# Where V's product and the gate's product of a span stand in TensorE's order, in a delta-rule layer on one core

## The chip, the cores and the metric

The kernel runs on one core of a Trainium2 chip. The metric is the device time of one execution in microseconds, as the median of several runs. A core has five engines with instruction streams of their own: TensorE (PE; its weight loads are PEld), VectorE (DVE), ScalarE (ACT), GpSimd (POOL) and SyncE (SP), which here only issues DMAs. They meet through semaphores alone.

## The reference, cut to what matters

The input is 16 sequences of 512 tokens with 512 features. Four layers follow each other: a delta-rule attention layer, a feed-forward layer with routed adapters, a softmax attention layer, and the feed-forward layer again. The change touches the first only:

```python
q = silu(x @ Wq.T).reshape(b, n, h, hd)          # 16 heads of 32
k = silu(x @ Wk.T).reshape(b, n, h, hd)
v = (x @ Wv.T).reshape(b, n, h, hd)
beta = 2.0 * jax.nn.sigmoid(x @ Wbeta.T)
k = k * jax.lax.rsqrt(jnp.sum(k * k, axis=-1, keepdims=True) + EPS)
# for every token:  pred = kt S;  delta = bt (vt - pred);  S = S + kt delta;  o = qt S
o = _delta_rule(q, k, v, beta).reshape(b, n, d)
gate = jax.nn.sigmoid(x @ Wg1.T @ Wg2.T)
og = (o * gate).reshape(b, n, h, hd)
rms = jax.lax.rsqrt(jnp.mean(og * og, axis=-1, keepdims=True) + EPS)
og = (og * rms).reshape(b, n, d) * g_norm
return og @ Wo.T
```

## The kernel before, in words

**Tiling.** A sequence is cut into two spans of 256 tokens, so there are 32 spans. A span has four chunks of 64 tokens. The recurrence over tokens is rewritten: within a chunk, the dependence of later tokens on earlier ones is a triangular matrix per head (`triangles`, stored in `tri`), whose inverse is computed on VectorE in 32x32 blocks (`invert`). Between chunks only the state S is carried, in four steps per span (`chain(c)` on TensorE, `advance(c)` on VectorE).

**Software pipeline.** `over_spans` calls `begin` for the first two spans and then one `step` per span on every engine. In one step each engine works on several spans at once: `now` is solved and chained; `ahead`, the next, is inverted on VectorE; `further`, two spans on, is projected on TensorE; `beyond` is loaded and normalised; `behind` gets its output product. 28 of the steps are alike in that all of these exist and the pipeline is full. The order within a step is written out by hand for each engine, in the functions `step` of the kernel text. The products of 128x128 weights (k, q, V, output) are split into three products of reduced-precision parts (`split3`, lines 38 to 42), so that their instructions carry the lines L40 to L42 in the profile.

**TensorE's order before**, in one step: transposes of the normalised x (`turned`), `solve_first`, k's first half, `solve_second`, k's second half, `solve_third`, q's first half, `solve_fourth`, g and beta, `query_corrections`, output's first half, `transitions`, q's second half, `without_state`, output's second half, `state_inputs`, and then chain(0), key_sums(0), chain(1), gate(0), chain(2), gate(1), chain(3), key_sums(1), output_sums, V(0), key_rows, triangles, V(1). `key_sums` sums the squares of k by a product with ones, `output_sums` those of the gated output, and `key_rows` transposes the normalised k.

**What passes between the engines at the end of a step.** VectorE multiplies the output of each chain step by the gate (L918). ScalarE squares it (L366). TensorE sums (L701). ScalarE takes Ln (L371) and Exp (L376), and VectorE applies the result (L925, `output`). Then VectorE masks the triangles, eight of them (L883), and normalises x of `beyond` (L835), for which `turned` waits. TensorE's second set of four triangle products waits for VectorE, because it uses the same four banks. k's norm goes the same way: `key_sums`, Ln and Exp on ScalarE (`k_inverse_norms`, L329 and L333), the product on VectorE (`normalise_k`, L848), `key_rows` on TensorE.

**PSUM banks.** Eight banks of 512 columns. BA, BB, BC and BD (0 to 3) are shared by the transposes, the projections, the gate, V, key_sums, key_rows and the output product, banks 4 to 7 by the solve, the chain, output_sums and the triangles. A projection waits until the last user of its bank has been copied out.

**ScalarE's function tables.** Silu and Tanh are in one table set, Ln and Exp in another. The kernel loads each ahead of its first use (L433, L443), so that there are two loads a step. ScalarE's other work is copying and splitting: `x_hi` (L299) from the transposes, V and k rows into `rhs`, the solve's results into `uw`. VectorE takes `x_lo` (L841) from `x_hi`, and k's projection needs both.

**SyncE's order.** `store` and `load_residual`, then `from_lanes` (the inverted blocks go to DRAM, L207, and return in eight loads as `inv_b`, L211), then `to_lanes` (beta out, L190; eight stores of `tri`, L196; beta and blocks back into lanes, L200 and L202). The queue issues them in this order, and each waits for its own semaphore.

Of the kernel before, what the change touches and what calls it, by code (L numbers as in the profile page):

```python
# [44 lines left out]
def delta_rule_layer(nc, dims, x_in, w_main, w_gb, w_g2, g_norm, ident_in, masks_in, ones_in, out):  # L45
# [9 lines left out]
    with ExitStack() as ctx:  # L55
# [227 lines left out]
        def _(act):  # L283
# [99 lines left out]
            def begin(first, second, third):  # L383
                load_x(*first)
                act.wait_ge(xn_ready, TS)
                load_x(*second)
                for span, following in ((first, None), (second, third)):
                    if following:
                        act.wait_ge(xn_ready, 2 * TS)
                        load_x(*following)  # L390
                    act.preload_act_table_set(SILU_SET)
                    turned(*span)
                    take_k(*span, 0)
                    take_k(*span, 1)
# [3 lines left out]
                    take_gate(*span)  # L398
                    act.preload_act_table_set(LN_EXP_SET)
                    k_inverse_norms(*span)  # L400
                    take_v(*span, 0)
                    take_v(*span, 1)
                    take_k_rows(*span)
                act.preload_act_table_set(SILU_SET)

            def step(behind, now, ahead, further, beyond):
# [19 lines left out]
                if further:  # L426
                    take_q(*further, 1)
                output_squares(*now, 0)
                output_squares(*now, 1)
                if further:  # L430
                    act.wait_ge(og_ready, at(*now, 4, 4))
                    take_gate(*further)
                act.preload_act_table_set(LN_EXP_SET)  # L433
                if further:
                    k_inverse_norms(*further)
                output_inverse_rms(*now)
                if further:
                    take_v(*further, 0)
                output_hi(*now)
                if further:  # L440
                    take_k_rows(*further)
                    take_v(*further, 1)
                    act.preload_act_table_set(SILU_SET)  # L443

# [7 lines left out]
        def _(pe):  # L452
# [11 lines left out]
            def turned(b, s, first=False):  # L464

                pe.wait_ge(xn_ready, at(b, s, TS, TS))
                if not first:
                    pe.wait_ge(v_ready, at(b, s, TS, -1))
# [18 lines left out]
            def project_gb(b, s, first=False):  # L487
                if not first:
                    pe.wait_ge(v_ready, at(b, s, TS, 0))
                for k in range(KT):  # L490
# [232 lines left out]
            def begin(first, second, third):  # L723
                for span in (first, second):
# [5 lines left out]
                    project_q(*span, 1)  # L730
                    key_sums(*span, 0)
                    project_gate(*span, 0)
                    project_gate(*span, 1)
                    key_sums(*span, 1)
                    project_v(*span, 0)
                    project_v(*span, 1)
                    key_rows(*span)
# [5 lines left out]
            def step(behind, now, ahead, further, beyond):  # L743
# [28 lines left out]
                if further:  # L772
                    project_gate(*further, 0)
                chain(*now, 2)
                if further:
                    project_gate(*further, 1, behind)
                chain(*now, 3)
                if further:
                    key_sums(*further, 1)
                output_sums(*now)  # L780
                if further:
                    project_v(*further, 0)
                    key_rows(*further)
                    pe.wait_ge(ln2_ready, at(*now, 2, 2))
                    triangles(*further, 0)
                    triangles(*further, 1)
                    project_v(*further, 1)

# [8 lines left out]
        def _(dve):  # L797
# [156 lines left out]
            def step(behind, now, ahead, further, beyond):  # L954
# [30 lines left out]
                advance(*now, 3)  # L985
                invert_ahead("values")
                if further:
                    normalise_k(*further)
                output(*now)
                if further:  # L990
# [874 lines left out]
```

## Time and profile before

| | |
|---|---|
| median of 3 runs | 5666.98 us (5666.64 to 5681.62) |
| profiled execution | 5643.14 us, span 5641.2 us |
| mean granted TensorE clock | 0.936 |
| PE busy | 4965.0 us, 88% |
| DVE busy | 3602.9 us, 64% |
| ACT busy | 2445.5 us, 43% |
| POOL busy | 706.2 us, 13% |

Times are in microseconds from the start of the span. A granted clock of 1.00 is 2.4 GHz and 0.50 is 1.2 GHz. The shares are averages over the whole program. The layer in question ends at about 2,100 us.

### The profile page before, as it was taken

The numbers are of one execution on the slowest core, as the hardware profiler recorded it, in microseconds if no ns is written. First come the engines' busy times: TensorE is split into PE (matmuls) and PEld (weight loads), VectorE is DVE, ScalarE is ACT, GpSimd is POOL, SyncE is SP. The second block draws the span as 40 slices with busy tenths as digits, with TensorE's granted clock in tenths as the row PEclk, the third lists the DMA queues.
The fourth block names the chain that finished last, engine by engine and source line by source line (L and its number), as shares of the span: only waits on it lengthen the run. The fifth ranks groups of instructions, "written<-read, shape, count | busy, mean of one in ns | idle before, by whom it ended". The sixth has DMA issues, their size and how long they took to land.

```text
span 5641.2 us, 152483 instructions
## 1 busy us (share of the span) xinstructions
PE 4965.0 (88%) x62928; PEld 3566.3 (63%) x62928; DVE 3602.9 (64%) x7842; ACT 2445.5 (43%) x4660; POOL 706.2 (13%) x917
## 2 busy tenths in 40 slices
PE   4899999999999949898898898998988988988988
PEld 4787777777787736556556556555565565565565
DVE  3676676676676637566566565675675665665756
ACT  2333433333433324354363453553543644634535
POOL 0000000000000001111112112111111111121121
PEclk8899999999999969999999999998999999999999
DMA  1222222222322220000000000000000000000000
GB/s 55 67 56 68 70 56 67 71 56 63 74 56 68 66 73 1 16 2 16 16 1 16 16 1 16 16 1 16 1 16 16 2 16 16 1 16 17 1 16 9
DMA packets 352741, 173.61 MB, mean 31 GB/s; under 512 B 300033, under 2 KB 300801, under 8 KB 351265
## 3 DMA queue, kind: packets, MB, share of 16 engines
q1 hardware_dynamic: 343056, 146.25, 9.7%
q10 hardware_dynamic: 8976, 17.30, 1.0%
q8 instruction: 519, 8.50, 0.6%
q14 instruction: 190, 1.55, 0.1%
HBM read 94.79 MB, written 67.63 MB: 29 GB/s over the span
## 4 chain that ended last, share of the span: by engine, by line
issue 30%; PE 21%; DVE 7%; POOL 3%; ACT 1%; DMA 0%; DVEq 0%; POOLq 0%; SPq 0%; ACTq 0%
PE row_psum L40 5%; PE row_psum L42 5%; PE row_psum L41 5%; DVE smax L1772 3%; POOL xs L1227 2%; PE row_psum L1356 1%; PE row_psum L1493 1%; DVE stats L1598 1%; PE row_psum L1460 1%; POOL rstd L1199 1%; PE row_psum L1461 1%; PE row_psum L1475 1%; DVE xr_lo L1627 1%; DVE xs L1701 1%; DVE probs L1609 0%
## 5 line engine op out<-in xcount | busy, mean ns | idle before, releaser
L1772 DVE TENSOR_REDUCE smax<-row_psum 128x1 f32<-128x512 f32 x2048 | 1263.7, 683 | 294.7 <-PE row_psum L1493 293.4
L1325 ACT ACTIVATE probs<-row_psum 128x512 f32<-128x512 f32 x2048 | 1078.3, 610 | 528.5 <-PE row_psum L1506 350.0
L1493 PE MATMUL row_psum<-k_stack,q_stack 128*128 128x512 f32 x2048 | 866.6, 434 | 28.3 <-DVE smax L1772 24.5
L1506 PE MATMUL row_psum<-q_stack,k_stack 128*128 128x512 f32 x2048 | 855.2, 428 | 29.2 <-ACT probs L1325 20.9
L1493 PEld LDWEIGHTS row_psum<-k_stack,q_stack 128*128 128x128 f32 x2048 | 395.0, 194 | 346.3 <-DVE smax L1772 251.4
L1506 PEld LDWEIGHTS row_psum<-q_stack,k_stack 128*128 128x128 f32 x2048 | 385.9, 191 | 292.8 <-ACT probs L1325 188.6
L1519 PE MATMUL row_psum<-probs,v_aug 128*32 128x512 f32 x4096 | 489.1, 598 | 0.0
L40 PE MATMUL row_psum<-wf_hi,xr_hi 128*128 128x320 f32 (+1 forms) x1024 | 328.2, 321 | 13.1 <-DVE xr_lo L1627 12.5
L868 DVE TENSOR_TENSOR lane_t<-lane_t,lane_p 128x30 f32<-128x30 f32 (+14 forms) x960 | 318.5, 332 | 32.9
L865 DVE TENSOR_TENSOR lane_p<-lane_t 128x30 f32<-128x30 f32 (+14 forms) x960 | 316.2, 329 | 23.5
L40 PE MATMUL span_bank<-x_hi,w_hi 128*128 128x256 f32 x1024 | 301.0, 294 | 29.7 <-DVE x_lo L841 29.2
L42 PE MATMUL row_psum<-wf_hi,xr_lo 128*128 128x320 f32 (+1 forms) x1024 | 325.1, 317 | 0.0
L41 PE MATMUL row_psum<-wf_lo,xr_hi 128*128 128x320 f32 (+1 forms) x1024 | 324.3, 317 | 0.0
L1356 PE MATMUL row_psum<-ident,probs 128*128 128x128 f32 x784 | 169.5, 371 | 172.9 <-DVE probs L1609 172.8
L41 PE MATMUL span_bank<-x_lo,w_hi 128*128 128x256 f32 x1024 | 288.6, 282 | 0.0
L42 PE MATMUL span_bank<-x_hi,w_lo 128*128 128x256 f32 x1024 | 288.1, 281 | 0.0
L1762 DVE RECIPROCAL av_rc<-row_psum 128x16 f32<-128x16 f32 x128 | 32.2, 252 | 397.8 <-PE row_psum L1566 397.8
L1227 POOL TENSOR_TENSOR xs<-xs,av_n 128x256 f32<-128x256 f32 x128 | 92.9, 726 | 1538.5 <-DVE av_n L1766 1538.5
L1245 ACT ACTIVATE xr_hi<-row_psum 128x512 fp32r<-128x512 f32 x196 | 112.0, 600 | 398.6 <-PE row_psum L1356 398.6
L1356 PEld LDWEIGHTS row_psum<-ident,probs 128*128 128x128 f32 x784 | 119.8, 187 | 223.8 <-DVE probs L1609 173.0
L263 POOL TENSOR_TENSOR o_lo<-og_both,o_hi 128x512 fp32r<-128x512 f32 x64 | 93.2, 1475 | 1323.1 <-DVE tri L883 1233.5
L1519 PEld LDWEIGHTS row_psum<-probs,v_aug 128*32 128x32 f32 x4096 | 108.5, 109 | 218.0 <-issue 173.8
(207 smaller groups left out, 9955.2 us busy)
## 6 DMA issues: line engine op xcount, KB each, us to landing
xs<-x SPq DMA_DIRECT2D x17, 1024.0 KB, 5.6
x_sp<-in_x ACTq DMA_DIRECT2D x33, 512.0 KB, 3.9
tri_dram<-tri SPq DMA_DIRECT2D x256, 64.0 KB, 2.1
lane_t<-tri_dram SPq DMA_DIRECT2D x32, 512.0 KB, 4.7
inv_dram<-lane_t SPq DMA_DIRECT2D x32, 512.0 KB, 2.6
inv_b<-inv_dram SPq DMA_DIRECT2D x256, 64.0 KB, 2.3
x_res<-in_x SPq DMA_DIRECT2D x32, 512.0 KB, 3.8
x<-x_res SPq DMA_DIRECT2D x32, 512.0 KB, 3.7
```

Of the source, the lines that this page charges most:

```text
L40: pe.matmul(out, a_hi, b_hi, start=first, stop=False)
L41: pe.matmul(out, a_hi, b_lo, start=False, stop=False)
L42: return pe.matmul(out, a_lo, b_hi, start=False, stop=last)
L865: mark(dve.tensor_tensor(prod, lane_t[:, 0:m, m:m + 1].to_broadcast([P, m, n]), lane_t[:, m:m + 1, m + 1:NB].to_broadcast([P, m, n]), ALU. ...
L868: mark(dve.tensor_tensor(lane_t[:, 0:m, m + 1:NB], lane_t[:, 0:m, m + 1:NB], prod, ALU.add))
L1227: pool.tensor_tensor(xq, xq, av_n[:, :, :, :].rearrange("p t h e -> p t (h e)"), ALU.add).then_inc(adot_added, 1)
L1325: act.activation(probs[:, h % PROBS, tt, :], ps[:, m % STACK_BANKS, :], ACT.Exp, scale=float(DH) ** -0.5).then_inc(exp_ready, 1)
L1356: last = pe.transpose(ps[:, t, P * k:P * k + P], xn[:, t, P * k:P * k + P], ident2[:, :])
L1493: pe.matmul(ps[:, STACK_BANKS + m % MAX_BANKS, :], q_stack[:, qt, P * st:P * st + P], k_stack[:, kv, :], start=True, stop=True).then_inc(m ...
L1506: pe.matmul(ps[:, m % STACK_BANKS, :], k_stack[:, kv, P * tt:P * tt + P], q_stack[:, qt, :], start=True, stop=True).then_inc(score_mm, 1)
L1519: last = pe.matmul(ps[32 * e:32 * e + 32, 6, :], v_aug[:, tt, h % NKV, :], probs[:, h % PROBS, tt, :], start=tt == 0, stop=tt == NT - 1)
L1772: dve.tensor_reduce(smax[:, g, st:st + 1], ps[:, STACK_BANKS + (NT * g + st) % MAX_BANKS, :], AX.X, ALU.max).then_inc(max_ready, 1)
```

## The change

On TensorE, V(0) moves to the place between chain(1) and chain(2), and V(1) to the place between chain(2) and chain(3), with key_sums(1) ahead of it. gate(0) moves behind output_sums, ahead of key_rows, and gate(1) behind the triangles, to the end of the step. The waits that protect banks BA and BB go along: V now waits for q and beta, the gate for V's copies, and the next span's transposes and g product for the gate's. On ScalarE, the load of the Ln and Exp table, V's copies and k's norms stand between the squares of the output; the load of the Silu and Tanh table, the copies of the key rows and the gate's Tanh stand at the end. On VectorE, `normalise_k` stands ahead of the inversion's last columns (`values`, two columns and the scaling) and no longer behind them. In `begin` the order of V and gate changes likewise, on TensorE and ScalarE. No instruction is added or removed.

```diff
 # ScalarE, step
                 take_transition(*now)
                 if further:
                     take_q(*further, 1)
+                act.preload_act_table_set(LN_EXP_SET)
+                if further:
+                    take_v(*further, 0)
                 output_squares(*now, 0)
+                if further:
+                    k_inverse_norms(*further)
+                    take_v(*further, 1)
                 output_squares(*now, 1)
-                if further:
+                output_inverse_rms(*now)
+                output_hi(*now)
+                if further:
+                    act.preload_act_table_set(SILU_SET)
                     act.wait_ge(og_ready, at(*now, 4, 4))
+                    take_k_rows(*further)
                     take_gate(*further)
-                act.preload_act_table_set(LN_EXP_SET)
-                if further:
-                    k_inverse_norms(*further)
-                output_inverse_rms(*now)
-                if further:
-                    take_v(*further, 0)
-                output_hi(*now)
-                if further:
-                    take_k_rows(*further)
-                    take_v(*further, 1)
-                    act.preload_act_table_set(SILU_SET)
 # TensorE, waits
-            def project_gate(b, s, n, behind=None):
+            def project_gate(b, s, n):
+                pe.wait_ge(v_ready, at(b, s, TS, n + 1))
                 if n == 0:
-                    pe.wait_ge(q_ready, at(b, s, 2, 1))
                     pe.wait_ge(g1_ready, at(b, s, 1, 1))
-                else:
-                    pe.wait_ge(beta_ready, at(b, s, 1, 1))
-                    if behind:
-                        pe.wait_ge(x2_ready, at(*behind, TS, CREDIT + TS))
...
-            def project_v(b, s, t):
-                pe.wait_ge(gate_ready, at(b, s, 2, t + 1))
+            def project_v(b, s, t, behind=None):
+                if t == 0:
+                    pe.wait_ge(q_ready, at(b, s, 2, 1))
+                else:
+                    pe.wait_ge(beta_ready, at(b, s, 1, 1))
+                    if behind:
+                        pe.wait_ge(x2_ready, at(*behind, TS, CREDIT + TS))
 # TensorE, step
                 chain(*now, 1)
                 if further:
+                    project_v(*further, 0)
+                chain(*now, 2)
+                if further:
+                    key_sums(*further, 1)
+                    project_v(*further, 1, behind)
+                chain(*now, 3)
+                output_sums(*now)
+                if further:
                     project_gate(*further, 0)
-                chain(*now, 2)
-                if further:
-                    project_gate(*further, 1, behind)
-                chain(*now, 3)
-                if further:
-                    key_sums(*further, 1)
-                output_sums(*now)
-                if further:
-                    project_v(*further, 0)
                     key_rows(*further)
                     pe.wait_ge(ln2_ready, at(*now, 2, 2))
                     triangles(*further, 0)
                     triangles(*further, 1)
-                    project_v(*further, 1)
+                    project_gate(*further, 1)
 # VectorE, step
                 advance(*now, 3)
+                if further:
+                    normalise_k(*further)
                 invert_ahead("values")
-                if further:
-                    normalise_k(*further)
                 output(*now)
```

## Rows read from the trace of the kernel before

**Rows 1.** Windows of core 0: stretch and its length, then busy us of each engine.
```profile
core 0: us, PE busy (x) PEld busy (x) DVE busy (x) ACT busy (x) POOL busy (x), PEclk, DMA share, GB/s
213.23:1902.70 1689.47, 1594.74 (x41105) 1320.38 (x41105) 1184.77 (x2912) 643.57 (x1121) 107.46 (x113) 0.97 0.26 65
970.70:981.00 10.30, 10.30 (x214) 7.13 (x215) 3.98 (x14) 0.67 (x2) 0.00 (x0) 0.57 0.18 55
```
**Rows 2.** Waits from 400 to 1950 us: who waited for whom, total, times, longest.
```profile
PE span_bank L40 <- DVE x_lo L841: 22.0, 25, 1.2
...
PE span_bank L691 <- issue: 18.0, 14, 2.4
```
**Rows 3.** Timeline of TensorE from 1036.9: start, us, line, idle before and releaser.
```profile
1037.00 1.13 PE L524 MATMUL span_bank<-g_beta,g 32*128 32x256 f32 x4
...
1039.98 0.45 PE L685 MATMUL span_bank<-state,gt 32*32 32x32 f32 x32
1040.85 1.12 PE L511 MATMUL span_bank<-sq,head_ones 128*128 128x512 f32 x2
1042.10 1.12 PE L701 MATMUL span_bank<-og_both,head_ones 128*128 128x512 f32 x2
...
1047.49 1.09 PE L539 MATMUL span_bank<-ident,kq 128*128 128x128 f32 x8 [0.62 <-DVE kq L848]
1048.52 5.03 PE L551 MATMUL span_bank<-kq 32*64 32x128 f32 x128
1053.48 0.50 PE L40 MATMUL span_bank<-w_hi,x_hi 128*128 128x512 f32 x1
...
1056.75 1.09 PE L474 MATMUL span_bank<-ident,r_norm 128*128 128x128 f32 x8 [0.20 <-DVE r_norm L835]
...
1060.55 0.36 PE L40 MATMUL span_bank<-x_hi,w_hi 128*128 128x256 f32 x1 [0.81 <-DVE x_lo L841]
...
1068.44 0.24 PE L577 MATMUL span_bank<-og_both,inv_b 32*32 32x64 f32 x1
```
**Rows 4.** Timeline of VectorE from 1040.9 to 1064.2, same columns.
```profile
1040.96 0.42 DVE L918 SCALAR_TENSOR_TENSOR og_both<-gate,span_bank 128x256 f32<-128x256 f32 x1
...
1043.55 0.20 DVE L874 COPY lane_t<-lane_b 128x32 f32<-128x32 f32 x1
1046.14 1.29 DVE L848 TENSOR_TENSOR kq<-kq,r_norm 128x512 f32<-128x512 f32 x2 [2.40 <-ACT r_norm L333]
1048.34 1.67 DVE L925 SCALAR_TENSOR_TENSOR og_both<-og_both,gnorm_half 128x256 f32<-128x256 f32 x4 [0.90 <-ACT og_both L376]
1049.93 4.87 DVE L883 TENSOR_TENSOR tri<-span_bank,masks 128x512 f32<-128x512 f32 x8
1054.71 1.98 DVE L835 TENSOR_SCALAR r_norm<-x_sp,mv,rstd 128x512 f32<-128x512 f32 x2
...
1063.96 0.18 DVE L856 TENSOR_SCALAR lane_b<-lane_b 128x32 f32<-128x32 f32 x1 [3.55 <-DMA lane_t<-tri_dram]
```
**Rows 5.** Timeline of ScalarE from 1046.5 to 1059.6, same columns.
```profile
1046.52 1.26 ACT L371 ACTIVATE og_both<-span_bank,eps_t 128x512 f32<-128x512 f32 x2
1047.66 1.16 ACT L376 ACTIVATE og_both<-og_both 128x512 f32<-128x512 f32 x2
...
1057.19 1.28 ACT L443 ACT_TABLE_LOAD   x1
1058.49 1.09 ACT L299 ACTIVATE x_hi<-span_bank 128x512 fp32r<-128x512 f32 x2
```
**Rows 6.** Timeline of SyncE's DMA issues from 1043 to 1064.2, same columns.
```profile
1046.40 4.05 SPq L211 DMA_DIRECT2D inv_b<-inv_dram  x8
...
1052.43 4.39 SPq L196 DMA_DIRECT2D tri_dram<-tri  x8
...
1058.34 0.34 SPq L202 DMA_DIRECT2D lane_t<-tri_dram  x1
```
**Rows 7.** The tile lane_t from 400 to 1900 us: time from issue to landing.
```profile
DMA to landing us min/median/max: 2.6/3.1/5.8
```
**Rows 8.** Page, DMA queues: packets, MB, share of 16 engines' span.
```profile
q8 instruction: 519, 8.50, 0.6%
```

More of the change, by code:

```diff
@@ L397, in begin @@
                     take_q(*span, 1)
-                    take_gate(*span)
+                    take_v(*span, 0)
+                    take_v(*span, 1)
                     act.preload_act_table_set(LN_EXP_SET)
                     k_inverse_norms(*span)
-                    take_v(*span, 0)
-                    take_v(*span, 1)
                     take_k_rows(*span)
-                act.preload_act_table_set(SILU_SET)
+                    act.preload_act_table_set(SILU_SET)
+                    take_gate(*span)
             def step(behind, now, ahead, further, beyond):
@@ L427, in step @@
                     take_q(*further, 1)
-                output_squares(*now, 0)
-                output_squares(*now, 1)
-                if further:
-                    act.wait_ge(og_ready, at(*now, 4, 4))
-                    take_gate(*further)
                 act.preload_act_table_set(LN_EXP_SET)
                 if further:
+                    take_v(*further, 0)
+                output_squares(*now, 0)
+                if further:
                     k_inverse_norms(*further)
+                    take_v(*further, 1)
+                output_squares(*now, 1)
                 output_inverse_rms(*now)
-                if further:
-                    take_v(*further, 0)
                 output_hi(*now)
                 if further:
+                    act.preload_act_table_set(SILU_SET)
+                    act.wait_ge(og_ready, at(*now, 4, 4))
                     take_k_rows(*further)
-                    take_v(*further, 1)
-                    act.preload_act_table_set(SILU_SET)
+                    take_gate(*further)
             def end(now):
@@ L467, in turned @@
                 if not first:
-                    pe.wait_ge(v_ready, at(b, s, TS, -1))
+                    pe.wait_ge(gate_ready, at(b, s, 2, -1))
                     pe.wait_ge(rhs_k_ready, at(b, s, TS, 0))
@@ L488, in project_gb @@
                 if not first:
-                    pe.wait_ge(v_ready, at(b, s, TS, 0))
+                    pe.wait_ge(gate_ready, at(b, s, 2, 0))
                 for k in range(KT):
@@ L526, in project_gate @@
                 last.then_inc(gate_proj, 1)
-            def project_v(b, s, t):
-                pe.wait_ge(gate_ready, at(b, s, 2, t + 1))
+            def project_v(b, s, t, behind=None):
+                if t == 0:
+                    pe.wait_ge(q_ready, at(b, s, 2, 1))
+                else:
+                    pe.wait_ge(beta_ready, at(b, s, 1, 1))
+                    if behind:
+                        pe.wait_ge(x2_ready, at(*behind, TS, CREDIT + TS))
                 for k in range(KT):
@@ L731, in begin @@
                     key_sums(*span, 0)
+                    project_v(*span, 0)
+                    project_v(*span, 1)
+                    key_sums(*span, 1)
                     project_gate(*span, 0)
                     project_gate(*span, 1)
-                    key_sums(*span, 1)
-                    project_v(*span, 0)
-                    project_v(*span, 1)
                     key_rows(*span)
@@ L985, in step @@
                 advance(*now, 3)
-                invert_ahead("values")
                 if further:
                     normalise_k(*further)
+                invert_ahead("values")
                 output(*now)
```

2 lines of the change are left out of this document (1 added, 1 removed).

## The prediction

> **What bounds the kernel now.** I read the waits of the stretch in which the layer runs evenly, then one period of it engine by engine, then the granted clock. The slices of the page put the change's layer into the first 2,100 us; the token layers behind it are untouched. Its steady part is 28 periods, 1689.47 us, so 60.3 us each, with TensorE busy for 94% of it [rows 1]. TensorE sets the period: what the change can win or lose is TensorE idle time and its clock. The waits show two kinds of idle time that matter [rows 2]: x_lo ends late (22.0 us over 25 periods, about 0.8 each), and "issue" at the chain (18.0 us in 14). The rows of one period, counted from the start of chain(3) at 1039.98 (t = 0), show the rest [rows 3]: output_sums at 2.12, a wait of 0.62 for kq ahead of key_rows, triangles from 8.54 to 13.50, V1 behind them to 16.57, a wait of 0.20 for xn, and turned at 16.77. That last wait is small, but it says that VectorE reaches this point together with TensorE. VectorE's rows [rows 4] give its own course: last gated output ready at 1.40, inversion done at 3.77, a hole until ScalarE has k's norms, normalise_k, another hole until ScalarE has the output's norms, output at 8.36, tri from 9.95 to 14.8, xn until 16.71. So the stretch from chain(3) to turned is already a chain through VectorE with V0 and V1 lying beside it as cover.
>
> **TensorE, chain(3) to turned.** Each V takes 3.07 us (1053.48 to the wait before 1056.75), 3.0 from start to start; a gate product 1.1, key_sums 1.1 [rows 3]. V0, V1 and key_sums(1) leave this stretch (7.1 us), both gates enter it (2.2): 4.9 to 5.0 us less work. The same work goes between the chain's steps, where TensorE is busy anyway; it costs there what it costs here. So the sum is about idle time alone.
>
> **The course through VectorE.** New order: og(3) at 1.40, Square, output_sums at 2.12 as before (the 0.72 between them is the Square); its first sum is there at 3.24, its second at about 4.1. ScalarE is free now: the table load and k's norms ran before. Ln of half a tile is 1.26/2, Exp 1.16/2 [rows 5]: Ln to 3.9, Ln to 4.8, the first Exp to 5.4. VectorE meanwhile: normalise_k 1.29 (its norms are ready, because key_sums(1) stands before V1), inversion 2.4, done at 5.1. Output starts at 5.5 instead of 8.36, 2.9 earlier, and tri, xn and turned follow at the same distances: tri 1.59 later, its eight products 4.8, xn 2.0. Turned starts at 13.9 instead of 16.77. TensorE would be through with its part at 0.87 + 1.75 + 1.1 + 1.03 + 4.96 + 1.1, about 10.8. So it stands idle for 3.1 us here (1.25 right behind chain(3), which key_sums(1) covered, and 1.8 before turned, which V1 covered) where it stood for about 1.1. **Price: +2.0 us a period.** Bounds: 1.5 if the output's norms come 0.5 earlier than I have them (the inversion ends at 5.1, so not more), 2.5 if the extra wait between engines comes in twice.
>
> **x_lo.** The table load at 1057.19 goes ahead of x_hi because V1's copy must come first [rows 5], and TensorE waits 0.81 at 1060.55 [rows 3]. In the new order the load stands behind output_hi (8.4 to 9.6), and the last gate's copy ends before turned starts. x_hi can follow the transposes, x_lo ends 2.5 after turned starts, and solve_first lasts until 3.0. **Gain: -0.8 a period**, between -0.8 and 0. The 0.62 for kq goes too, but it is in the stretch already counted.
>
> **SyncE's queue.** The inversion is ready 1.3 later after chain(3), since normalise_k stands ahead of its last columns. Before, the eight loads of inv_b were issued by 10.47 and tri's eight stores could begin with tri at 12.45 [rows 6]. Now the loads end at 11.8, beta's store at 12.3, and the stores of tri, whose first four tiles are ready at 9.5, wait in the queue: eight at 0.5 end at 16.3, which is 2.4 behind turned where it was 0.07. lane_t's load then leaves at turned + 3.9 instead of + 1.59. It landed 5.62 later here [rows 4, 6], and VectorE needs 2.5 more until the first corrected right side is written. That is turned + 12.0; TensorE comes to solve_third at + 11.69 now [rows 3] and would at + 10.9: a wait of 1.1. Where the transfer takes the median of 3.1 [rows 7] there is none. I take 0.3, bounds 0 and 1.1. inv_b itself lands about 1 us before solve_first wants it; I take nothing, with 0.5 as the far end.
>
> **Issue stalls.** They come once a period around state_inputs and chain(0), ahead of V0's new place, so I leave them. Later small ones in the chain could be covered: -0.1, bounds -0.7 and 0. The page has instruction transfers of 8.50 MB in 519 packets, 16.4 KB each [rows 8]. The Trainium skill (Runtime: NRT & Kernel Launch, "Instruction fetch mechanics") says that instructions come in blocks of 16 KiB, fetched one ahead; the packets agree. By that rule V between chain steps gives the fetch time in the densest stretch, and the stalls that fall behind V0 would go (0.7 a period at most): the sum would be 17 us lower, still above before.
>
> **Clock.** Over the 28 periods the mean is 0.97, so about 6% of the time (102 us) ran at 1.2 GHz; 970.70 to 981.00 is such a stretch, in the chain [rows 1]. Of the 102 us, stretches of 1 us show 85 in 13 chains (this one is 10.2 of them) and 17 near the triangles of 5 periods. The periods that had it are 2 us longer than those that had none: it costs some 30 us altogether. V in the chain should halve the first part (-14). The new stretch from triangles to solve_first has 32-row products, a gate, 1.8 idle and 32x32 products in a row, and will throttle more often (+14, between 0 and +50). I take zero for both together.
>
> **Sum.** 28 x (2.0 - 0.8 + 0.3 - 0.1) = +39 us. The begin part, the two steps around the steady part and the last two, which project nothing, I put at nothing: in begin the same products and table loads stand in another order, and the last steps keep theirs. The profiled execution took 5643.1 us (span 5641.2), so it would take 5682. The median of the runs shown is 5667.0, 23.8 above it; so I predict 5706.
>
> **Rivals.**
> - *The clock decides, and the kernel is faster.* V fills the chain with full 128x128 products, so the clock stays at 2.4 GHz there, and the triangles' stretch doesn't fall either. Price: 30 us saved of clock, 3 of stalls, 22 of x_lo, against at most 1.5 x 28 = 42 through VectorE: 5654; with the stalls covered by 0.7 a period, 5637. It decides from the point where clock and stalls save over 1.3 us a period. For it: 13 of 28 periods had a throttled chain. Against: the first falls come right behind the issue stall, before V0. 0.12.
> - *Even.* The course through VectorE costs only 1.5 and lane_t is never late: 28 x (1.5 - 0.8 - 0.3) = +11 us, 5678. For it: before, the kq wait and the xn wait already showed slack of both kinds. 0.22.
> - *The clock falls behind the triangles in nearly every period.* Seven us of narrow products and waiting, then narrow products again: 5 us more at 1.2 GHz a period, some 1.7 us each, less the 14 saved: +70 to +75 in all, 5738. Against: in 23 of the 28 periods the triangles passed at 1.0. The Trainium skill (TensorE: Matmul & The Clock Gate, "What's actually happening") has it that the throttled state is the default and activity releases it; the fall behind an idle gap at the chain agrees, and the rule speaks against a change that opens gaps. 0.16.
> - *My likeliest case*, 5690 to 5725: 0.50.
>
> The own range of the likeliest is 5690 to 5725. The range I give, 5656 to 5744, takes in the even case, most of the last, and the upper part of the clock's. What a measurement here can tell from no change is about 0.3%, 17 us. Faster by more: 0.12; within: 0.23; slower by more: 0.65.
>
> **What would show it.** In the changed trace: x_lo's wait gone from TensorE's list; a new idle of about 1.2 before output_sums, released by the Square, and one near 1.8 before the transposes, released by xn; VectorE's output 5.5 behind chain(3); SyncE's tri stores ending after turned; lane_t waits of VectorE about as long or longer, and now and then a wait of solve_third for og_both. Wrong if the wait for xn stays under 0.5 us, or if the mean clock of the steady part moves by more than 0.02.

## The result, and the profile after

| | before | after |
|---|---|---|
| median | 5666.81 us (5657.61 to 5681.62, 6 runs) | 5790.34 us (5784.20 to 5792.54, 6 runs) |
| profiled execution | 5643.14 us, span 5641.2 | 5790.76 us, span 5788.8 |
| mean granted clock | 0.936 | 0.916 |

The ratio is 1.0215 with a 95% interval of [1.0201, 1.0229]. The kernel is slower, as forecast, but by 123 us and not by 39. It lies outside the range.

The two profiled spans differ by 147.6 us, more than the medians, because the profiled execution of before (5643.14) was faster than each of its six timed runs; the 4.26 us a period below may be too large by up to 0.8 for that reason. By stage: the 28 steady periods take 1808.8 us instead of 1689.5, which is 64.60 each instead of 60.34: +119.3. The stretch ahead of them takes 226.6 instead of 213.2: +13.4. The end of the layer behind them adds 8.2, and the token layers, which are unchanged, 6.7. So four fifths of it is 4.26 us a period, and the rest of this section is about one period.

Windows of core 0 of the kernel after: the steady part, the wait ahead of turned, ten microseconds from the start of turned, and ten within a chain.

```profile
core 0: us, PE busy (x) PEld busy (x) DVE busy (x) ACT busy (x) POOL busy (x), PEclk, DMA share, GB/s
226.62:2035.39 1808.77, 1671.87 (x41105) 1403.23 (x41105) 1185.19 (x2912) 665.19 (x1120) 106.43 (x113) 0.91 0.24 60
1064.42:1066.53 2.11, 0.01 (x1) 0.00 (x0) 2.06 (x3) 0.60 (x1) 1.83 (x2) 0.82 0.76 118
1066.50:1076.50 10.00, 9.97 (x95) 9.47 (x96) 1.38 (x2) 2.39 (x4) 1.10 (x1) 0.52 0.63 150
1106.00:1116.00 10.00, 8.80 (x228) 6.14 (x217) 4.80 (x17) 2.38 (x5) 0.00 (x0) 1.00 0.32 108
```

The steady part ran at a mean clock of 0.91 where it was 0.97 [rows 1]. That is not idle time: PE busy grew by 77 us for the same 41105 instructions. The next two rows show where. The clock fell while TensorE stood idle ahead of turned (0.82 over that wait), and from turned on it ran ten microseconds at a mean of 0.52, that is, nearly all of them at 1.2 GHz, and passed 95 matmuls. The ten microseconds behind turned in the period of [rows 3] had a clock of 1.00 and passed 235. Over the whole steady part 314 us were at 1.2 GHz, where it was 102. Of these, 259 lie behind the start of turned and 31 ahead of it, about 10.4 us in every one of the 28 periods; in 24 of them the clock fell within the wait. Only 24 us lie in the chain (7 periods), where it was 85 (14 periods).

Waits of the kernel after, from 400 to 2050 us:

```profile
PE span_bank L474 <- DVE r_norm L835: 54.4, 26, 2.1
PE span_bank L702 <- ACT og_both L366: 30.6, 26, 1.2
...
DVE lane_b L856 <- DMA lane_t<-tri_dram: 181.7, 26, 8.2
```

Both new waits are there, 2.1 us for xn and 1.2 for the Square, and x_lo's and kq's [rows 2, 3] are gone. Timeline of TensorE, one period; chain(3) starts at 1052.50:

```profile
1052.50 0.45 PE L686 MATMUL span_bank<-state,gt 32*32 32x32 f32 x32
1054.61 1.99 PE L702 MATMUL span_bank<-og_both,head_ones 128*128 128x512 f32 x4 [1.18 <-ACT og_both L366]
1056.53 1.13 PE L520 MATMUL span_bank<-g_beta,g 32*128 32x256 f32 x4
1057.58 1.09 PE L540 MATMUL span_bank<-ident,kq 128*128 128x128 f32 x8
1058.60 4.77 PE L552 MATMUL span_bank<-kq 32*64 32x128 f32 x128
1063.30 1.13 PE L520 MATMUL span_bank<-g_beta,g 32*128 32x256 f32 x4
1066.53 1.97 PE L474 MATMUL span_bank<-ident,r_norm 128*128 128x128 f32 x8 [2.11 <-DVE r_norm L835]
1068.43 3.62 PE L562 MATMUL span_bank<-rhs,inv_b 32*32 32x64 f32 x64
...
1081.73 0.24 PE L570 MATMUL span_bank<-uw,tri 32*32 32x64 f32 x1
```

The last row is in solve_third, 15.2 behind turned. The kernel before, for comparison, in its solve_first:

```profile
1057.77 1.98 PE L561 MATMUL span_bank<-rhs,inv_b 32*32 32x64 f32 x64
```

The transposes of turned take 1.97 us where they took 1.09 [rows 3], and solve_first 3.62 for its 64 products where it took 1.98: they are the first things to run behind the wait of 2.11, and they run at half the clock. Timeline of VectorE:

```profile
1053.47 0.42 DVE L918 SCALAR_TENSOR_TENSOR og_both<-gate,span_bank 128x256 f32<-128x256 f32 x1
1053.81 1.29 DVE L848 TENSOR_TENSOR kq<-kq,r_norm 128x512 f32<-128x512 f32 x2
...
1057.26 0.20 DVE L874 COPY lane_t<-lane_b 128x32 f32<-128x32 f32 x1
1057.87 1.67 DVE L925 SCALAR_TENSOR_TENSOR og_both<-og_both,gnorm_half 128x256 f32<-128x256 f32 x4 [0.42 <-ACT og_both L376]
1059.74 4.88 DVE L883 TENSOR_TENSOR tri<-span_bank,masks 128x512 f32<-128x512 f32 x8 [0.20 <-PE span_bank L552]
1064.53 1.94 DVE L835 TENSOR_SCALAR r_norm<-x_sp,mv,rstd 128x512 f32<-128x512 f32 x2
...
1076.84 0.18 DVE L856 TENSOR_SCALAR lane_b<-lane_b 128x32 f32<-128x32 f32 x1 [6.98 <-DMA lane_t<-tri_dram]
```

Answering to [rows 4], the last gated output is ready 1.39 behind chain(3) (1.40 before), normalise_k follows at once, the inversion is done 4.96 behind (3.77 before), the output starts at 5.37 (8.36 before), and xn ends at 13.97. Timeline of ScalarE, answering to [rows 5]:

```profile
1057.22 1.14 ACT L376 ACTIVATE og_both<-og_both 128x512 f32<-128x512 f32 x2
1060.75 1.28 ACT L440 ACT_TABLE_LOAD   x1
```

And SyncE's issues, answering to [rows 6]:

```profile
1060.10 4.04 SPq L211 DMA_DIRECT2D inv_b<-inv_dram  x8
1064.72 4.48 SPq L196 DMA_DIRECT2D tri_dram<-tri  x8
1069.25 2.70 SPq L200 DMA_DIRECT2D lane_b<-beta_dram  x1
1073.67 0.34 SPq L202 DMA_DIRECT2D lane_t<-tri_dram  x1
```

The loads of inv_b end at 1064.1, where tri had its first tiles ready at about 1060.4. tri's stores therefore end at 1069.2, 2.7 behind turned, beta's load takes 2.7 more of the queue, and lane_t's load leaves 7.14 behind turned; before it left 1.59 behind. In the median period the stores end 4.6 behind turned. Yet TensorE has no wait for the corrected right sides in the list above.

### The profile page after: what moved, and what is told of

Same layout as the page of the kernel before. It is cut to its first block, busy times and chain, and to the rows that moved or that the text cites. A ratio compares the mean times of both kernels' runs of the same rounds, so it can differ in the third digit from the quotient of the medians.

```text
span 5788.8 us, 152483 instructions
## 1 busy us (share of the span) xinstructions
PE 5060.6 (87%) x62928; PEld 3663.7 (63%) x62928; DVE 3604.2 (62%) x7842; ACT 2467.6 (43%) x4660; POOL 705.0 (12%) x917
## 3 DMA queue, kind: packets, MB, share of 16 engines
q10 hardware_dynamic: 8976, 17.30, 1.1%
## 4 chain that ended last, share of the span: by engine, by line
issue 29%; PE 20%; DVE 7%; POOL 3%; ACT 1%; DMA 0%; DVEq 0%; POOLq 0%; SPq 0%; ACTq 0%
PE row_psum L40 5%; PE row_psum L42 5%; PE row_psum L41 5%; DVE smax L1772 3%; POOL xs L1227 2%; PE row_psum L1356 1%; PE row_psum L1493 1%; DVE stats L1598 1%; POOL rstd L1199 1%; PE row_psum L1460 1%; PE row_psum L1461 1%; PE row_psum L1475 1%; DVE xr_lo L1627 1%; DVE xs L1701 0%; DVE probs L1609 0%
## 5 line engine op out<-in xcount | busy, mean ns | idle before, releaser
L40 PE MATMUL row_psum<-wf_hi,xr_hi 128*128 128x320 f32 (+1 forms) x1024 | 328.5, 321 | 13.7 <-DVE xr_lo L1627 13.4
L40 PE MATMUL span_bank<-x_hi,w_hi 128*128 128x256 f32 x1024 | 327.1, 319 | 3.9 <-DVE x_lo L841 3.2
L41 PE MATMUL span_bank<-x_lo,w_hi 128*128 128x256 f32 x1024 | 311.2, 304 | 0.0
L42 PE MATMUL span_bank<-x_hi,w_lo 128*128 128x256 f32 x1024 | 309.3, 302 | 0.0
```

Of the source, the lines that this page charges most:

```text
L40: pe.matmul(out, a_hi, b_hi, start=first, stop=False)
L41: pe.matmul(out, a_hi, b_lo, start=False, stop=False)
L42: return pe.matmul(out, a_lo, b_hi, start=False, stop=last)
```

## The experiments

Each period length is the steady part over 28. The ratios are to the kernel before, run on the same chip; each kernel has 4 to 7 runs. A period comes from one profiled execution, which can lie some 10 us, 0.4 a period, from the median of its kernel.

**Fill the gap, wide.** The disputed points are the fall of the clock at turned and what stands behind it. Here six products of V's shape, whose result nobody reads, stand between the triangles and gate(1), where TensorE only waited. They are extra work.

```diff
                     triangles(*further, 0)
                     triangles(*further, 1)
+                    pe.wait_ge(v_ready, at(*further, TS, TS))
+                    for k in range(2):
+                        split3(pe, BB[:, :], x_hi[:, k, P:2 * P], x_lo[:, k, P:2 * P],
+                               w_hi[:, 2, k, :], w_lo[:, 2, k, :], k == 0, k == 1)
                     project_gate(*further, 1)
```

> The changed kernel with work that is thrown away: six products of 128x128 by 512 columns (V's own operands) into bank BB between the triangles and gate(1), 1.5 us a step, where TensorE stood idle for 2.1 us ahead of the transposes. Nothing is left out. Theory (clock): the changed kernel lost 119 us over the 28 periods, and only about 35 of that is idle time; the rest is the granted clock, which falls at the transposes in each period, because narrow products and then a wait stand ahead of them. With wide products there the clock stays up in most periods: 40 to 85 us faster than the changed kernel, 5705 to 5750, and the wait for xn shrinks from 2.10 to about 0.6 us. Rival (idle time and order alone; the clock is a by-product that costs little): the filler goes into the wait and changes nothing, 5785 to 5795.

Measured: 5798.13 us against 5660.96, ratio 1.0247 [1.0224, 1.0271]; period 64.66. Its steady part in one window, its waits, and SyncE's issues in the same period (turned at 1066.00):

```profile
225.09:2035.62 1810.53, 1634.99 (x41273) 1354.49 (x41273) 1179.00 (x2912) 665.54 (x1121) 106.64 (x113) 0.97 0.24 60
```
```profile
PE span_bank L570 <- DVE og_both L897: 74.9, 28, 3.8
PE span_bank L702 <- ACT og_both L366: 32.9, 28, 1.2
PE span_bank L474 <- DVE r_norm L839: 14.3, 28, 0.5
DVE lane_b L860 <- DMA lane_t<-tri_dram: 234.5, 28, 9.4
```
```profile
1059.58 5.42 SPq L211 DMA_DIRECT2D inv_b<-inv_dram  x8
1065.58 6.00 SPq L196 DMA_DIRECT2D tri_dram<-tri  x8
1071.62 0.50 SPq L200 DMA_DIRECT2D lane_b<-beta_dram  x1
1073.35 0.34 SPq L202 DMA_DIRECT2D lane_t<-tri_dram  x1
```

The clock is back at 0.97 and the wait for xn shrank from 2.1 to 0.5. But the time did not move, which neither the theory nor the rival had. In place of the slow stretch TensorE now waits 2.7 us in each of the 28 periods ahead of solve_third (L570 here), for the right side that VectorE corrects only after lane_t has landed. The clock is one cost, the late return another, and the second seems to be hidden under the first. The new wait has a price beyond its own length. This is solve_third in the same period, and the clock just behind it:

```profile
1079.90 0.21 PE L570 MATMUL span_bank<-uw,tri 32*32 32x64 f32 x1 [2.98 <-DVE og_both L897]
```
```profile
1081.20:1084.60 3.40, 3.40 (x61) 3.23 (x50) 3.33 (x10) 1.08 (x2) 0.00 (x0) 0.50 0.02 5
```

In 18 of the 28 periods the clock falls at this place, 2.6 us a period in all. In the kernel after it falls there in none.

**Fill the gap, narrow.** gate(1)'s two products, twice over, in the same place:

```diff
+                    pe.wait_ge(v_ready, at(*further, TS, TS))
+                    pe.wait_ge(g1_ready, at(*further, 1, 1))
+                    for g in (0, 1, 0, 1):
+                        pe.matmul(BB[:, SPAN * g:SPAN * g + SPAN], g2[:, P * (2 + g):P * (3 + g)], g1, start=True, stop=True)
                     project_gate(*further, 1)
```

> The changed kernel with the same place filled by narrow work that is thrown away: gate(1)'s own product (32 rows of the array, 256 columns) two times more, 4 matmuls, about 2.1 us a step. Theory A (waiting brings the clock down): it helps as much as wide products do, 40 to 85 us faster than the changed kernel. Theory B (the clock falls because the array is hardly used, whether TensorE waits or runs narrow products): no help, within 10 us of the changed kernel, 5780 to 5800, with the clock still falling near the transposes in every period. I hold B at 0.6.

Measured: 5808.78 us, ratio 1.0266 [1.0242, 1.0290], period 65.43. The steady part:

```profile
225.91:2058.06 1832.15, 1753.84 (x41329) 1466.44 (x41329) 1186.43 (x2912) 665.08 (x1120) 107.54 (x113) 0.90 0.24 60
```

TensorE waits only 0.11 a period for xn now, so it is hardly idle ahead of turned, and the clock still falls: 0.90. It falls up to 5 us ahead of turned, where narrow products run. This is the expectation's theory B, with a period 0.8 longer than in the kernel after and a time 9 us above its range. So in this kernel the idle time by itself is not what brings the clock down: the wide products in its place held it, the gate's narrow ones did not.

**V(1) back as cover.** V(1) returns behind the triangles, gate(1) goes ahead of output_sums, gate(0) behind it, V(0) stays in the chain; ScalarE's copies and the waits for the banks follow.

```diff
                 chain(*now, 2)
                 if further:
                     key_sums(*further, 1)
-                    project_v(*further, 1, behind)
                 chain(*now, 3)
+                if further:
+                    project_gate(*further, 1, behind)
                 output_sums(*now)
                 if further:
                     project_gate(*further, 0)
...
                     triangles(*further, 0)
                     triangles(*further, 1)
-                    project_gate(*further, 1)
+                    project_v(*further, 1)
```

> Half of the change: V(0) stays between chain(1) and chain(2) and the early norms stay, but V(1) is back behind the triangles; gate(1) stands between chain(3) and output_sums, where TensorE waited 1.2 us for the Square, and gate(0) behind output_sums. All work is done. By the rows of before: 1.9 us of work leaves the stretch from chain(3) to the transposes, which becomes 2.8 shorter, and x_lo's wait of 0.8 goes: 1.7 us less a period than before, 48 us in all, plus some of the clock's 30 us in the chain. Theory (V(1) was the cover of VectorE's course and kept the clock up ahead of the transposes): 5590 to 5630, faster than the kernel before. Rival (the clock falls because the stretch without wide products became longer on the whole): the triangles' stretch is still 9 us without a split product, the clock falls in most periods, 5650 to 5720.

Measured: 5716.81 us, ratio 1.0106 [1.0080, 1.0131], period 61.87. Steady part and waits:

```profile
232.69:1965.09 1732.40, 1592.20 (x41104) 1318.98 (x41105) 1180.47 (x2912) 658.90 (x1121) 107.56 (x113) 0.97 0.25 63
```
```profile
PE span_bank L572 <- DVE og_both L896: 62.8, 27, 3.9
PE span_bank L704 <- ACT og_both L366: 11.4, 28, 0.4
```

The clock holds, the Square's wait falls from 1.18 to 0.41 and xn's to 0.18, because real work stands in both gaps. Half of the loss goes: 56 us are left of 123. The time lies in the rival's range, but not by the rival's mechanism. The same wait at solve_third, 2.2 us a period, stays, since nothing was done about lane_t.

**GpSimd's part of the output, later.** In the kernel after, GpSimd starts on the output's low part when tri is written, just when VectorE makes xn.

```diff
                     inverse_std(*beyond)
-                    pool.wait_ge(tri_ready, at(*further, TS * HPT, TS * HPT))
+                    pool.wait_ge(xn_ready, at(*beyond, TS, TS))
                 output_lo(*now)
```

> The changed kernel with one wait changed: GpSimd's o_lo starts when both halves of xn are written, not when the triangles are. The second of VectorE's two xn instructions took 1.4 us where the first took 0.54, while GpSimd's o_lo ran. Theory: that is the end of VectorE's course, for which the transposes wait, so xn comes 0.85 us earlier, the wait of 2.10 becomes 1.25, and the period shortens by at least that: 24 us faster, 5760 to 5770; with a part of the clock's loss too if the length of the wait matters, down to 5720. Rival (the transposes are held by something else, or the pair is slow for another reason): no change, 5785 to 5795.

Measured: 5755.58 us, ratio 1.0171 [1.0146, 1.0197], period 63.64. VectorE's xn in one period, then the waits:

```profile
1056.82 0.99 DVE L835 TENSOR_SCALAR r_norm<-x_sp,mv,rstd 128x512 f32<-128x512 f32 x2
```
```profile
PE span_bank L474 <- DVE r_norm L835: 31.6, 29, 1.2
```

The pair of instructions takes 0.99 us instead of 1.94, and the wait for xn 1.1 instead of 2.1. The 0.96 us a period that this saves is nearly all that the kernel gains. The clock hardly moves (0.92): it still falls, in all 28 periods, around a gap of 1.1. The Trainium skill (SBUF — State Buffer, "SBUF: two separate sides") has it that VectorE and GpSimd share a port pair as an exclusive lock, which a GpSimd instruction, or a VectorE instruction of certain kinds (in a 2-port mode or with two SBUF inputs), keeps for its whole length while the other blocks. The trace of the kernel after agrees: VectorE's second xn instruction, which starts 0.29 us behind GpSimd's first, takes 1.49 us instead of 0.54 and ends 0.28 behind the end of GpSimd's. No run shows in which mode VectorE ran it.

**The inversion earlier.** The last columns, which stood behind chain(2) and chain(3), are all done behind chain(1). The inversion is then over before the last gated output, and SyncE gets the blocks sooner. The empty stages are skipped.

```diff
-                           inputs=range(23, 26), chain0=range(26, 27), chain1=range(27, 28), chain2=range(28, 29),
-                           values=range(29, NB - 1))
+                           inputs=range(23, 26), chain0=range(26, 27), chain1=range(27, NB - 1), chain2=(),
+                           values=())
```

Three kernels carry it: the kernel after, the one with the wide filler, and the one with V(1) as cover.

> The changed kernel with the last columns of the inversion and its scaling moved from behind the chain into the place between advance(1) and advance(2), where VectorE now waits 2.6 us for V(0) on TensorE. SyncE's loads of inv_b are then through before the triangles begin, and tri's stores don't wait behind them. Theory (two costs that lie beside each other: the clock's, from the transposes to k's first product, and lane_t's late return, which would hold solve_third at 13.7 us behind the transposes): in the changed kernel the slow clock brings TensorE to solve_third only at 15.1, so an earlier lane_t changes nothing, 5780 to 5795. Rival (the late return costs time of its own): 30 us or more faster, under 5760.

> Both at once: the wide filler ahead of gate(1), work that is thrown away, which kept the clock up, and the early end of the inversion. Theory (each of the two costs hides the other): the wait of 2.68 us for the corrected right side goes, 75 us less than the filler alone: 5710 to 5735. Rival (solve_third is held by x's load or by something else that the filler makes late, not by SyncE's order): the wait stays over 1.5 us, 5770 to 5800.

> V(1) back behind the triangles, gate(1) between chain(3) and output_sums, and the early end of the inversion. All work is done. Theory: the wait of 2.24 us a period for the corrected right side goes, 60 us less than without the early inversion: 5640 to 5665, level with the kernel before or a little faster. Rival (the rest of the difference to the kernel before is the clock, which still falls somewhere in each period): 5690 or more.

Measured: alone 5772.51 us against 5651.62, 1.0221 [1.0197, 1.0244], period 64.62. With the filler 5668.01 us, 1.0038 [1.0023, 1.0053], period 60.60. With V(1) as cover 5600.25 us, 0.9921 [0.9891, 0.9950], period 58.21. The steady part, alone:

```profile
226.20:2035.60 1809.40, 1679.32 (x41104) 1408.42 (x41105) 1188.90 (x2912) 665.44 (x1120) 106.47 (x113) 0.91 0.24 60
```

With the filler, steady part and waits:

```profile
227.49:1924.34 1696.85, 1603.24 (x41272) 1326.71 (x41273) 1181.30 (x2912) 662.27 (x1121) 106.60 (x113) 0.99 0.25 64
```
```profile
PE span_bank L702 <- ACT og_both L366: 32.9, 28, 1.2
PE span_bank L474 <- DVE r_norm L839: 13.3, 26, 0.5
```

With V(1) as cover:

```profile
231.14:1860.88 1629.74, 1560.97 (x41104) 1292.10 (x41105) 1182.03 (x2912) 656.41 (x1121) 107.47 (x113) 0.99 0.26 67
```

Together with the first experiment and the kernel after these make a table of two by two, in us a period:

| | inversion as in the change | inversion earlier |
|---|---|---|
| gap empty | 64.60 | 64.62 |
| gap filled, wide | 64.66 | 60.60 |

Each cure alone is worth nothing, and both together 4.0 us a period, 112 us in all. The medians, as differences to the kernel before on the same chip, say the same: 123 us with neither, 121 with the earlier inversion, 137 with the filler, 16 with both. With both, no wait for og_both at solve_third is left in the list. In the median period of this kernel tri's stores end at turned + 0.05 and lane_t's load leaves at + 1.6, as in the kernel before [rows 6]. This settles the cause: two costs of about 4 us lie beside each other behind turned, and each hides the other.

Both forecasts with the earlier inversion were too small. The filler was to gain 75 us by it and gained 114 in the steady part (64.66 less 60.60), and V(1) as cover was to gain 60 and gained 102 (61.87 less 58.21). For the filler the difference is mostly the clock behind the wait. Of its 4.06 us a period, 2.7 lie between turned and solve_third, which is the wait itself, and 1.5 between solve_third and chain(0) (24.96 against 23.44). In that second stretch 2.3 us a period ran at 1.2 GHz with the wait and none without it, and issue stalls took 0.3 more.

**k's norm back behind the last columns.** The wide filler stays; VectorE's order is that of before.

```diff
                 advance(*now, 3)
+                invert_ahead("values")
                 if further:
                     normalise_k(*further)
-                invert_ahead("values")
                 output(*now)
```

> The kernel with the wide filler (work that is thrown away) and one part of the change undone: normalise_k stands behind the inversion's last columns again, so that the inversion is ready 1.3 us earlier and SyncE's queue is free 1.3 us earlier. Theory (SyncE's queue is what holds lane_t): the wait for the corrected right side shrinks from 2.7 to 1.4 us, 36 us less than with the filler alone, 5755 to 5770. Rival (k's norm has no part in it): within 10 us of the filler alone, 5785 to 5805.

Measured: 5738.01 us, ratio 1.0169 [1.0148, 1.0190], period 62.91.

```profile
PE span_bank L570 <- DVE og_both L897: 42.9, 26, 4.2
```

The place of k's norm alone is worth 1.75 us a period (64.66 less 62.91) once the clock holds at turned: 1.3 us of normalise_k ahead of the inversion's end put SyncE's loads and stores back. The wait shrinks to 1.5, near the 1.4 of the forecast. The gain is 49 us in the steady part and not 36, with the clock falling behind the shorter wait in 9 periods instead of 18. Undoing it isn't enough. VectorE's output now starts 5.4 behind chain(3) and no longer 8.4, so tri and turned are early while the inversion is not.

**The best of it, and half a filler.** The first is the kernel with V(1) as cover and the earlier inversion, with GpSimd later as well:

```diff
-                    pool.wait_ge(tri_ready, at(*further, TS * HPT, TS * HPT))
+                    pool.wait_ge(xn_ready, at(*beyond, TS, TS))
```

> V(1) behind the triangles, the early end of the inversion, and GpSimd's o_lo behind xn, all work done. In the version without the last edit the transposes waited only 0.19 us a period for xn, since V(1) covers VectorE's course. Theory (V(1), not VectorE, ends last there): 0 to 5 us faster than that version, 0.3 to 1.0% faster than the kernel before, 5590 to 5635 where before is 5652. Rival (xn is late in more than the waits show, as where the same edit gave 35 us to the changed kernel): 20 us or more below it.

Measured: 5595.71 us against 5654.11, ratio 0.9890 [0.9873, 0.9906], period 58.29. Both kernels are beaten, by 1.1% and, by the two ratios, by 3.2%. Against the version without GpSimd's edit (0.9921 [0.9891, 0.9950]) there is no difference to tell: with V(1) as cover, xn had been waited for by only 0.19 a period.

The second is the kernel with filler and earlier inversion, with three wide products for six:

```diff
-                    for k in range(2):
+                    for k in range(1):
                         split3(pe, BB[:, :], x_hi[:, k, P:2 * P], x_lo[:, k, P:2 * P],
-                               w_hi[:, 2, k, :], w_lo[:, 2, k, :], k == 0, k == 1)
+                               w_hi[:, 2, k, :], w_lo[:, 2, k, :], k == 0, k == 0)
```

> The filler with the early end of the inversion, but three wide products, 0.75 us a step, where there were six (work that is thrown away). Theory (what counts is how much wide work stands between the triangles and the transposes): with 0.75 us of it the clock falls in part of the periods, mean clock of the steady part 0.93 to 0.98, 5690 to 5760. Rival (any wide work resets it): as with six, 5660 to 5680. Rival (no threshold is reached with three): as with none, 5765 to 5785.

Measured: 5813.62 us, ratio 1.0273 [1.0253, 1.0292], period 64.10. Steady part and the stretch of the token layers:

```profile
227.01:2021.80 1794.79, 1686.49 (x41189) 1404.27 (x41189) 1187.82 (x2912) 664.21 (x1120) 106.51 (x113) 0.92 0.24 61
2190.00:5813.00 3623.00, 3148.25 (x15952) 2057.33 (x15952) 2236.27 (x4502) 1692.42 (x3371) 582.81 (x779) 0.92 0.04 12
```

Three products, some 0.75 us of them, do not hold the clock (0.92), six do (0.99), and the difference is 3.5 us a period although the six are 0.7 us more work. The clock falls at turned in 25 of the 28 periods. The time is outside all three forecasts, but 47 us of it come from the token layers (see the last section). Without them it would be near 5766, and the clock and the period too are close to those of the rival "as with none".

## Why the prediction was wrong in size

Point by point, by its own steps:

- **TensorE sets the period; the moved work costs the same in its new place.** The first is right: at a mean clock of 0.99 the period with V(1) as cover and the earlier inversion is 58.2. The moved work added 4.2 us a period between chain(1) and chain(3), where 4.9 to 5.0 were counted. Before, 1.1 us a period of that stretch ran at the slow clock, and now 0.15.
- **The course through VectorE, +2.0.** The mechanism and the waits were right, the net was less. Forecast for the output's start behind chain(3) 5.5, measured 5.37; for turned 13.9, measured 14.03; for the two new waits 1.25 and 1.8, measured 1.18 and 2.09 over the 28 periods. The waits for kq and xn that they replace were 0.8 in the rows read (0.62 and 0.20; "about 1.1" was not a sum of rows) and 0.6 on average. But chain(3) to turned was 17.30 on average before, not the 16.77 of the period read, and became 3.3 shorter, while the moved work cost 4.2: the two together are +0.95.
- **x_lo, -0.8.** Right: the wait, 0.89 a period on average, is gone from the list, and turned to solve_third is 1.0 shorter where the clock holds (10.88 for 11.90).
- **SyncE's queue, +0.3 (bounds 0 and 1.1).** The mechanism was right, the size was not. Forecast: tri's stores end 2.4 behind turned and lane_t's load leaves at + 3.9. Measured in the median period: + 4.6 and + 7.1. The loads of the inverted blocks end later than I had them (1.4 ahead of turned and not 2.1), and the eight stores take 5.5 there instead of 4.3 before. Why they take longer isn't isolated; ScalarE's queue issues the load of the next x right among them, which I left out of the count. The wait was foreseen at 0 to 1.1 and is 2.7 once nothing else covers it. With the fall of the clock behind it the period loses 4.1. In the kernel as changed it shows nothing, because TensorE comes later still.
- **Clock, 0 (bounds -14 and +50 us).** This is the step that failed. Its first half held: the chain's share fell from 85 to 24 us. Its second half, +14, was put far too low. The rival "the clock falls behind the triangles in nearly every period", which had 0.16, is what came. It falls in all 28. That rival's price was too small as well: 5 us more at 1.2 GHz and 1.7 us a period. Measured were 9.2 us behind turned in each period, where before there were none. And the 1.7 goes by the price read before (30 us lost for 102 slow ones, most of them in the chain), where a slow stretch lies beside VectorE's steps. Behind turned TensorE has 32x32 products and k's projection in a row with nobody to wait for, and the slow stretch cost there 4.2: TensorE reaches solve_third at turned + 15.1, against + 10.87 in the kernel with cover and earlier inversion. My + 10.9 was right for a clock that holds.
- **Issue stalls, -0.1.** Right in size: TensorE's waits for "issue" in the steady part are 1.6 us a period where they were 1.8. Most are still in the chain.
- **Begin and the end of the layer, 0.** Wrong by 13.4 and 8.2 us of the profiled spans. The mean clock of the first 213 us is 0.82 where it was 0.86, so a part is the same fall of the clock; how much was not tried.

As a sum for a steady period, from the places of TensorE's instructions: turned to solve_third went from 11.90 to 15.08, which is -1.0 (x_lo's wait) and +4.2 (clock). chain(1) to turned went from 22.13 to 23.08, the +0.95 above. The rest, solve_third to chain(1), added 0.14. Together that is the measured 4.26 within rounding, where the forecast had 1.4. SyncE's queue adds nothing to it, and the clock is the step that makes the difference.

Two of the stated signs deserve a look. "Wrong if the mean clock of the steady part moves by more than 0.02" is what happened (0.97 to 0.91). And the wait of solve_third for og_both, which I named as a sign, was absent in the changed kernel although its cause was there.

The Trainium skill (TensorE: Matmul & The Clock Gate, "What's actually happening") says that the throttled state is the default and activity releases it. I had it speak against the change and gave it 0.16; the 28 falls around a gap of 2.1 us agree, and so does the 0.99 with wide products in the gap. The narrow filler is not told by that sentence: TensorE was busy for 96% of the steady part, and the clock was 0.90.

## What to carry to other kernels

Work that only seems to fill time beside another engine may be what holds TensorE's clock: before moving wide products away from a stretch of narrow ones, price the stretch behind them at 1.2 GHz, in full where TensorE is the bound there. When an experiment removes a cost that the trace plainly shows and the time stays, look at what arrives just before the removed cost ended, and remove both. A wait that is laid open in this way can bring the clock down behind it and so cost more than its length (4.1 for 2.7 here). Who brings a consumer forward (turned by 2.7 us in the periods shown, 3.3 on average) must bring forward the instruction that feeds the head of its transfers' queue too, or at least not push it back.

## What of the hardware was not expected

- A gap of 2.1 us behind narrow products brought the clock down in every period; with 0.11 us of gap and four more narrow products it fell as well (0.90), with three wide products in 25 of 28 (0.92), with six not (0.99 in the kernel with the inversion earlier). In the kernel after each fall began between 2.6 us ahead of turned and 0.2 behind it and lasted 10.2 us (13.7 once), over k's wide products too.
- A wait of 2.7 us at solve_third, just behind k's wide products, brought the clock down in 18 of 28 periods, mostly for 3.4 us.
- Two xn instructions on VectorE took 1.94 us beside GpSimd's work and 0.99 without it.
- In the kernel with three filler products the token layers, whose code is unchanged, took 3624.7 us where the kernel with six took 3577.2. All its four runs lie within 5801.8 to 5819.0, so it belongs to the kernel and not to one execution. In the other eleven profiles these layers took 3576 to 3588. In TensorE's waits the difference that stands out is an issue stall. From 2100 us on, for six products and then for three:

```profile
PE row_psum L40 <- issue: 3.5, 1, 3.5
```
```profile
PE row_psum L40 <- issue: 21.4, 7, 3.3
```

Seven stalls of some 3 us instead of one are 18 us of the 47, and the mean clock of that stretch is 0.92 against 0.93. The two kernels differ by three instructions a step ahead of it, so the place of the loops' code in memory may be a cause, but no run isolates it.
